# The first chunk's first two pairs of feed-forward products, issued among attention's last groups

## The chip, the cores and the metric

One core of a Trainium2 chip runs the whole program in one launch. The metric is the device time in microseconds, from the first to the last instruction of the core, and less is better. TensorE (PE) does the matrix products, with a queue of its own for loading weights (PEld); VectorE (DVE), ScalarE (ACT) and GpSimd (POOL) do the rest; SyncE (SP) issues most of the DMAs. Each engine is given its own list of instructions, and the lists meet only at semaphores.

## The reference

One transformer layer on x of 4096 tokens by 256 channels, all in float32:

```python
q, k, v = split_heads(x @ Wq.T + bq), ...      # 16 heads of 16
q, k = rope(q), rope(k)
att = softmax(where(tril, q @ k.T / 4, -inf))
x1 = layernorm(x + (att @ v) @ Wo.T + bo)
h = silu((x1 @ w1.T) * s1) * ((x1 @ w2.T) * s2)   # 256 -> 1024
h = gelu((h @ h1.T) * hs1)                        # 1024 -> 1024
h = gelu((h @ h2.T) * hs2)                        # 1024 -> 1024
out = layernorm(x1 + (h @ w3.T) * s3)             # 1024 -> 256
```

## The kernel before

The program has four stages, one behind the other on every engine: `project` (q, k, v), `attend` (attention), `widen` (the feed-forward layers w1/w2 and h1) and `narrow` (h2, w3 and the last norm).

**Attention.** The work is cut into 32 blocks (4 quads of heads, 8 chunks of 512 queries) and 576 groups of 128 keys; the last quad goes through its chunks from the longest to the shortest, so that its last blocks have 12, 8 and 4 groups. In a group PE computes four key units (`key_unit`, lines 513 and 516, three banks `at_key`), ACT turns each into probabilities with Exp (line 648), and PE multiplies the probabilities of the group before by the values (`values`, line 532, bank `at_o`). Beside this PE computes row units (line 499, four banks `at_row`), whose maxima DVE takes. The row units run ahead of the keys: they end with group `rows_done` = 555, and from group 556 on the four row banks are free. When a block is complete, ACT copies `at_o` out (`take_out`, line 639) between two groups' probabilities, and SP stores it.

**The preparation of the first chunk** (class `Prepare`, for chunk 0, whose attention is complete early) is written into attention's last groups. DVE multiplies the attention's output by the inverse denominators (`scale`, L843, `fr_o`). PE multiplies by Wo in four pieces (`project`, L820), one behind each of groups 559 to 562, into row banks 0 and 1. DVE adds, normalises and writes x1 (`norm`, L859 to L876, with one step on POOL). PE transposes x1 behind group 571 (`turn`, L829), again into row banks 0 and 1. DVE splits the transposed x1 into a high and a low part (`split_x1t`, L884 and L886, tile `fr_x1t`) and splits w1 and w2 in the same manner (`split_weight`, L732 and L734).

**The feed-forward stage** (`widen`) goes through eight chunks. In a chunk there are eight pairs k of products: product w1 and product w2 for 128 hidden channels each, six matrix instructions of 512 columns apiece (L970), into banks 2(k mod 2) and 2(k mod 2)+1 of four. ACT applies Silu to the first bank of a pair (L1011), DVE multiplies it with the second (L1032, here called the gate) and splits the product in two more passes (L1036, L1038). From k = 2 on a pair's banks have to be free again:

```python
if k >= 2:
    pe.wait_ge(pair_taken, n * FK + k - 1)
```

Then come the eight products of the h1 layer (L970 too, but from `wi_h_h`), whose results ACT takes with Gelu (L1017). The h1 weights are loaded by SP in eight pieces after the last block's output has been stored, and DVE splits them: in the first chunk one piece behind the gate of k = 3, one behind that of k = 5, the rest behind k = 7. Silu, Gelu and Exp need different tables in ACT, and an ACT_TABLE_LOAD stands ahead of the first use of each.

Banks of PSUM: `project`, `attend` and `widen` each open their own tensors, on the same eight banks of the chip.

Of the kernel before, what the change touches and what calls it, by code (L numbers as in the profile page):

```python
# [57 lines left out]
def project(nc, block, keep, io, qp_d, kp_d, v_d, front):  # L58
# [6 lines left out]
    with ExitStack() as ctx:  # L65
# [20 lines left out]
        main_ps = [ctx.enter_context(nc.psum_tensor(f"pr_main{i}", [P, CH], F32)) for i in range(3)]  # L86
        rot_ps = [ctx.enter_context(nc.psum_tensor(f"pr_rot{i}", [P, CH], F32)) for i in range(2)]
# [263 lines left out]
def attend(nc, block, keep, io, qp_d, kp_d, v_d, max_d, o_d, front, prep, projected):  # L351
# [16 lines left out]
    with ExitStack() as ctx:  # L368
# [20 lines left out]
        row_ps = [ctx.enter_context(nc.psum_tensor(f"at_row{i}", [P, CH], F32)) for i in range(RING_R)]  # L389
# [94 lines left out]
        def _(pe):  # L484
# [57 lines left out]
            for g, (n, j) in enumerate(groups):  # L542
# [349 lines left out]
def widen(nc, block, keep, io, h2_d, front, prep, attended):  # L892

    with ExitStack() as ctx:
# [14 lines left out]
        fb = [ctx.enter_context(nc.psum_tensor(f"wi_f{i}", [P, CH], F32)) for i in range(4)]  # L909
# [4 lines left out]
        pair_ready = sem("pair_ready")  # L914
# [47 lines left out]
        def _(pe):  # L962
            def product(bank, w, moving, count, cols, made=None, before=0):

                m = 0
                for c in range(count):
                    if made is not None:
                        pe.wait_ge(made, before + c + 1)
                    for a, b in ((0, 0), (0, 1), (1, 0)):
                        last = nc.tensor.matmul(bank[:, :], w[a][:, c, cols], moving(b, c),  # L970
                                                start=(m == 0), stop=(m == 3 * count - 1))
                        m += 1
# [373 lines left out]
```

## Time and profile before

| | |
|---|---|
| three runs | 2834.88, 2837.89, 2838.22 us; median 2837.89 |
| profiled execution | 2839.76 us; its span 2837.9 us |
| PE busy | 2739.1 us, 97% of the span |
| DVE, ACT, POOL busy | 67%, 48%, 4% |
| mean granted TensorE clock | 0.982 |
| attention ends, feed-forward begins on PE | 1806.3 and 1807.2 us from the span's start |

The profile lists, for every instruction, when it started, how long it took, how long its engine had been idle and what ended that idle time. Times below are counted from the span's start. A busy PE is counted with modelled ends, so that where products stand close behind one another only their starts say what one costs.

### The profile page before, as it was taken

The numbers are of one execution on the slowest core, as the hardware profiler recorded it, in microseconds if no ns is written. First come the engines' busy times: TensorE is split into PE (matmuls) and PEld (weight loads), VectorE is DVE, ScalarE is ACT, GpSimd is POOL, SyncE is SP. The second block draws the span as 40 slices with busy tenths as digits, with TensorE's granted clock in tenths as the row PEclk, the third lists the DMA queues.
The fourth block names the chain that finished last, engine by engine and source line by source line (L and its number), as shares of the span: only waits on it lengthen the run. The fifth ranks groups of instructions, "written<-read, shape, count | busy, mean of one in ns | idle before, by whom it ended". The sixth has DMA issues, their size and how long they took to land.

```text
span 2837.9 us, 39313 instructions
## 1 busy us (share of the span) xinstructions
PE 2739.1 (97%) x14880; PEld 1429.8 (50%) x14880; DVE 1902.2 (67%) x4001; ACT 1350.5 (48%) x2641; POOL 112.4 (4%) x151
## 2 busy tenths in 40 slices
PE   8889899999999999999999999999999998999998
PEld 4423233333333333333333332588888887888886
DVE  7889799888888887888887775633333352443343
ACT  3426566777776776777777776411211111001100
POOL 3302000010000020000000000000000000000000
PEclk9979899999999999999999999999999999999999
DMA  7734400017000053000001000311111132111100
GB/s 207 192 79 61 63 3 3 3 23 86 3 4 5 6 63 56 5 3 3 1 3 39 19 3 10 105 67 57 57 60 58 42 126 102 45 63 70 44 15 23
DMA packets 94732, 133.46 MB, mean 47 GB/s; under 512 B 30582, under 2 KB 68214, under 8 KB 90838
## 3 DMA queue, kind: packets, MB, share of 16 engines
q1 hardware_dynamic: 81436, 96.25, 10.6%
q0 software_dynamic: 5472, 23.34, 6.7%
q10 hardware_dynamic: 7648, 11.54, 1.4%
q8 instruction: 108, 1.77, 0.3%
q14 instruction: 68, 0.56, 0.1%
HBM read 83.77 MB, written 47.32 MB: 46 GB/s over the span
## 4 chain that ended last, share of the span: by engine, by line
PE 68%; issue 21%; DVE 6%; DMA 2%; ACT 1%; ACTq 1%; SPq 0%; POOL 0%; another core or an unknown queue 0%; POOLq 0%; DVEq 0%
PE at_o L532 18%; PE at_row L499 16%; PE at_key L513 15%; PE wi_f L970 15%; DVE at_segmax L584 3%; DVE fr_masked L580 1%; ACT at_probs L648 1%; DMA maxima<-at_maxrows 1%; PE at_key L516 1%; PE wi_p L820 1%; PE pr_main L130 1%; DVE pr_parts L251 1%; PE pr_rot L141 1%; PE pr_v L151 0%; DVE pr_full L247 0%
## 5 line engine op out<-in xcount | busy, mean ns | idle before, releaser
L648 ACT ACTIVATE at_probs<-at_key 128x512 f32<-128x512 f32 (+3 forms) x2304 | 1128.0, 567 | 523.6 <-PE at_key L513 367.9
L584 DVE TENSOR_REDUCE at_segmax<-at_row 128x1 f32<-128x512 f32 x1792 | 1143.1, 684 | 183.4 <-PE at_row L499 179.3
L513 PE MATMUL at_key<-fr_q_stack,fr_k_stack 99*128 99x512 bf16 (+3 forms) x1152 | 416.3, 366 | 14.9 <-DMA fr_q_stack<-maxima 10.6
L499 PE MATMUL at_row<-fr_k_stack,fr_q_stack 96*128 96x512 bf16 (+3 forms) x1152 | 406.0, 377 | 19.1 <-POOL at_values L429 13.3
L513 PE MATMUL at_key<-at_q_stack,at_k_stack 99*128 99x512 bf16 (+3 forms) x1152 | 403.9, 366 | 6.9 <-ACT at_probs L648 6.3
L499 PE MATMUL at_row<-at_k_stack,at_q_stack 96*128 96x512 bf16 (+3 forms) x1152 | 408.7, 365 | 1.7 <-DVE at_segmax L584 1.1
L532 PE MATMUL at_o<-at_probs,at_values 128*32 128x512 f32 (+3 forms) x2304 | 288.7, 574 | 0.0
L532 PE MATMUL at_o<-at_probs,fr_values 128*32 128x512 f32 (+3 forms) x2304 | 287.9, 572 | 0.0
L580 DVE CUSTOM_DVE_ANT_0 fr_masked<-at_row,fr_causal 128x384 f32<-128x384 f32 (+3 forms) x512 | 243.7, 483 | 54.7 <-PE at_row L499 54.3
L499 PEld LDWEIGHTS at_row<-fr_k_stack,fr_q_stack 96*128 96x128 bf16 x1152 | 110.6, 99 | 316.9 <-DVE at_segmax L584 159.7
L499 PEld LDWEIGHTS at_row<-at_k_stack,at_q_stack 96*128 96x128 bf16 x1152 | 110.8, 98 | 307.7 <-DVE at_segmax L584 163.5
L1205 ACT ACTIVATE na_h3f<-na_h,na_hs 128x512 f32<-128x512 f32 x64 | 44.1, 690 | 405.8 <-PE na_h L1175 405.8
L1175 PE MATMUL na_h<-na_h_h,fr_h2w_h 128*128 128x512 f32 x512 | 203.8, 398 | 9.0 <-DVE na_h_l L1220 9.0
L1175 PE MATMUL na_h<-na_h_l,fr_h2w_h 128*128 128x512 f32 x512 | 203.6, 398 | 0.0
L1175 PE MATMUL na_h<-na_h_h,fr_h2w_l 128*128 128x512 f32 x512 | 203.4, 397 | 0.0
L970 PE MATMUL wi_f<-wi_h_h,wi_h1w_h 128*128 128x512 f32 x512 | 201.4, 393 | 0.0
L970 PE MATMUL wi_f<-wi_h_l,wi_h1w_h 128*128 128x512 f32 x512 | 199.3, 389 | 0.0
L970 PE MATMUL wi_f<-wi_h_h,wi_h1w_l 128*128 128x512 f32 x512 | 199.3, 389 | 0.0
L1017 ACT ACTIVATE wi_h<-wi_f,fr_hs 128x512 f32<-128x512 f32 x64 | 44.1, 689 | 324.6 <-PE wi_f L970 324.6
L1227 DVE CAST na_h_h<-na_h3f 128x512 fp32r<-128x512 f32 x64 | 27.3, 426 | 246.1 <-ACT na_h3f L1205 246.1
L513 PEld LDWEIGHTS at_key<-at_q_stack,at_k_stack 99*128 99x128 bf16 x1152 | 111.8, 98 | 158.0 <-ACT at_probs L648 95.1
L513 PEld LDWEIGHTS at_key<-fr_q_stack,fr_k_stack 99*128 99x128 bf16 x1152 | 113.0, 98 | 112.6 <-ACT at_probs L648 37.2
(116 smaller groups left out, 2733.5 us busy)
## 6 DMA issues: line engine op xcount, KB each, us to landing
hidden<-wi_h SPq DMA_DIRECT2D x64, 256.0 KB, 2.0
na_h2f<-hidden SPq DMA_DIRECT2D x8, 1024.0 KB, 7.7
q_parts<-pr_parts SPq DMA_DIRECT2D x48, 128.0 KB, 2.4
k_parts<-pr_parts SPq DMA_DIRECT2D x48, 128.0 KB, 3.3
at_q_stack<-q_parts POOLq DMA_DIRECT2D x48, 128.0 KB, 23.7
at_k_stack<-k_parts POOLq DMA_DIRECT2D x12, 512.0 KB, 28.1
values<-pr_vals SPq DMA_DIRECT2D x32, 136.0 KB, 4.1
outputs<-at_outs SPq DMA_DIRECT2D x128, 34.0 KB
```

The costliest lines, as they stand in the source:

```text
L130: last = nc.tensor.matmul(main_ps[g % 3][:, :], w[m // DH][:, c, cols], xt[:, n % BUFS, c, :], start=(c == 0), stop=(c == DH - 1))
L141: nc.tensor.matmul(rot_ps[g % 2][:, :], turn[:, :], lin[:, g % 3, :], start=True, stop=True).then_inc(rot_ready, 1)
L499: last = nc.tensor.matmul(bank[:, 0:w], qst[u][0:SROWS, c, h, i * P:(i + 1) * P], kst[u][0:SROWS, h, s * CH:s * CH + w], start=True, stop= ...
L513: last = nc.tensor.matmul(bank[:, q0:CH], kst[u][0:SROWS + PARTS, h, j * P:(j + 1) * P], qst[u][0:SROWS + PARTS, c, h, q0:CH], start=True, ...
L532: last = nc.tensor.matmul(o_ps[32 * h:32 * h + 32, q0:CH], vq[u][:, at:at + 32], probs[:, g % RING_P, h, q0:CH], start=(j == 0), stop=(g = ...
L580: nc.vector.tensor_tensor_reduce(out=masked[:, diagonal[r] % 2, 0:w], in0=row_ps[r % RING_R][:, 0:w], in1=causal[:, CH - w:CH], scale=1.0, ...
L584: nc.vector.tensor_reduce(segmax[:, n % 2, h * TPC + i, s:s + 1], row_ps[r % RING_R][:, 0:w], op=ALU.max, axis=AX.X).then_inc(rows_taken, 1)
L648: nc.scalar.activation(probs[:, g % RING_P, h, q0:CH], key_ps[m % RING_K][:, q0:CH], ACT.Exp).then_inc(probs_ready, 1)
L970: last = nc.tensor.matmul(bank[:, :], w[a][:, c, cols], moving(b, c), start=(m == 0), stop=(m == 3 * count - 1))
L1017: nc.scalar.activation(h2[:, k % 2, :], fb[k % 4][:, :], ACT.Gelu, scale=front.hs[:, k:k + 1]).then_inc(hid_taken, 1)
L1175: last = nc.tensor.matmul(hb[k % 4][:, :], h2w[a][:, c, cols], h2[b][:, c, :], start=(m == 0), stop=(m == 3 * FK - 1))
L1205: nc.scalar.activation(h3f[:, k % 2, :], hb[k % 4][:, :], ACT.Gelu, scale=hs[:, k:k + 1]).then_inc(hid_taken, 1)
```

## The change

PE now issues the pairs k = 0 and k = 1 of chunk 0 behind attention's groups 569 and 572, and `widen` starts chunk 0 with k = 2. The four banks that were `at_row`, `wi_f` and so on in the separate stages are one set, `front.banks`, for the whole program, and the chip's banks stay the same as before. The preparation uses only banks 2 and 3, with Wo's products behind groups 557 to 560 and the transposes behind group 566, since pair 0 writes banks 0 and 1, and pair 1 banks 2 and 3. On DVE the split of w1 stands ahead of the norm, and that of w2 ahead of `split_x1t`. The number of instructions stays as it was. ACT's and DVE's code for Silu and gate doesn't move: it still stands behind their part of attention.

```diff
+EARLY_PAIRS = 2
...
-        row_ps = [ctx.enter_context(nc.psum_tensor(f"at_row{i}", [P, CH], F32)) for i in range(RING_R)]
+        row_ps = front.banks
...
-                i = g - rows_done - 4
-                if i == 0:
+                after = g - rows_done
+                if after == 2:
                     pe.wait_ge(rows_taken, len(rows))
-                if 0 <= i < TPC:
-                    prep.project(pe, 0, i, row_ps[i // 2])
-                if i == 12:
-                    prep.turn(pe, 0, row_ps)
+                if 2 <= after < 2 + TPC:
+                    prep.project(pe, 0, after - 2, row_ps[2 + (after - 2) // 2])
+                if after == 11:
+                    prep.turn(pe, 0, row_ps[2:4])
+                if after in (14, 17):
+                    pe.wait_ge(prep.x1t_ready, DH)
+                    pe.wait_ge(prep.w_split, 4)
+                    first_layer(nc, pe, front, 0, (after - 14) // 3)
             values(NG - 1)
...
-            prep.norm(dve, 0, row_ps)
-            for i, (high, low) in enumerate((front.w1, front.w2)):
-                dve.wait_ge(prep.w_loaded[i], 16)
-                split_weight(dve, high[:, :, :], low[:, :, :], front.w_raw[i][:, :, :], prep.w_split, 2 * i)
-                if i == 0:
-                    prep.split_x1t(dve, 0, row_ps)
+            dve.wait_ge(prep.w_loaded[0], 16)
+            split_weight(dve, front.w1[0][:, :, :], front.w1[1][:, :, :], front.w_raw[0][:, :, :], prep.w_split, 0)
+            prep.norm(dve, 0, row_ps[2:4])
+            dve.wait_ge(prep.w_loaded[1], 16)
+            split_weight(dve, front.w2[0][:, :, :], front.w2[1][:, :, :], front.w_raw[1][:, :, :], prep.w_split, 2)
+            prep.split_x1t(dve, 0, row_ps[2:4])
...
+def first_layer(nc, pe, front, n, k):
+
+    cols = slice(k * P, (k + 1) * P)
+    x1t = front.x1t[n % 2]
+    product(nc, pe, front.banks[2 * (k % 2)], front.w1, lambda b, c: x1t[:, b, c, :], DH, cols)
+    product(nc, pe, front.banks[2 * (k % 2) + 1], front.w2, lambda b, c: x1t[:, b, c, :], DH, cols).then_inc(front.pair_ready, 1)
...
-                for k in range(FK):
-                    cols = slice(k * P, (k + 1) * P)
+                for k in range(EARLY_PAIRS if n == 0 else 0, FK):
                     if k >= 2:
                         pe.wait_ge(pair_taken, n * FK + k - 1)
                     elif n > 0:
                         pe.wait_ge(hid_taken, (n - 1) * FK + 6 + 2 * k)
-                    product(fb[2 * (k % 2)], front.w1, lambda b, c: x1t[:, b, c, :], DH, cols)
-                    product(fb[2 * (k % 2) + 1], front.w2, lambda b, c: x1t[:, b, c, :], DH, cols).then_inc(pair_ready, 1)
+                    first_layer(nc, pe, front, n, k)
```

How this stands in the engines' queues. On PE, before, values of group 568 are followed straight by the keys of group 570 (`at_o` is the values' bank, 32x512 x4 the four heads):

```order
L513 MATMUL at_key<-at_q_stack,at_k_stack 128x384
L516 MATMUL at_key<-at_mask,at_ident 128x128
L532 MATMUL at_o<-at_probs,at_values 32x512 x4
L513 MATMUL at_key<-at_q_stack,at_k_stack 128x256
L516 MATMUL at_key<-at_mask,at_ident 128x128
L513 MATMUL at_key<-at_q_stack,at_k_stack 128x256
```

In the change the same place, behind group 569, holds the twelve instructions of pair 0 (L744 is `product`, 4 rows of 3; `fr_bank` is the common name of the four banks):

```order
L533 MATMUL at_o<-at_probs,at_values 32x512 x4
L744 MATMUL fr_bank<-fr_x1t_66,fr_w_h 128x512 x2
L744 MATMUL fr_bank<-fr_x1t_66,fr_w_l 128x512
L744 MATMUL fr_bank<-fr_x1t_66,fr_w_h 128x512 x2
L744 MATMUL fr_bank<-fr_x1t_66,fr_w_l 128x512
L744 MATMUL fr_bank<-fr_x1t_66,fr_w_h 128x512 x2
L744 MATMUL fr_bank<-fr_x1t_66,fr_w_l 128x512
L744 MATMUL fr_bank<-fr_x1t_66,fr_w_h 128x512 x2
L744 MATMUL fr_bank<-fr_x1t_66,fr_w_l 128x512
L514 MATMUL at_key<-at_q_stack,at_k_stack 128x256
L517 MATMUL at_key<-at_mask,at_ident 128x128
L514 MATMUL at_key<-at_q_stack,at_k_stack 128x256
```

Pair 1 stands in the same way behind group 572. What moved is the order alone: both pairs come from the stage's boundary, which on PE looked as follows before (values of groups 574 and 575, the branch into `widen`, pair 0):

```order
L513 MATMUL at_key<-at_q_stack,at_k_stack 128x128
L516 MATMUL at_key<-at_mask,at_ident 128x128
L532 MATMUL at_o<-at_probs,at_values 32x256 x4
L532 MATMUL at_o<-at_probs,at_values 32x128 x4
L961 UNCONDITIONAL_BRANCH
L970 MATMUL wi_f<-fr_x1t_66,fr_w_h 128x512 x2
L970 MATMUL wi_f<-fr_x1t_66,fr_w_l 128x512
L970 MATMUL wi_f<-fr_x1t_66,fr_w_h 128x512 x2
```

In the change the row behind the branch is the first of pair k = 2, which waits for `pair_taken`:

```order
L514 MATMUL at_key<-at_q_stack,at_k_stack 128x128
L517 MATMUL at_key<-at_mask,at_ident 128x128
L533 MATMUL at_o<-at_probs,at_values 32x256 x4
L533 MATMUL at_o<-at_probs,at_values 32x128 x4
L988 UNCONDITIONAL_BRANCH
L744 MATMUL fr_bank<-fr_x1t_66,fr_w_h 128x512 x2
L744 MATMUL fr_bank<-fr_x1t_66,fr_w_l 128x512
```

The names are the same as before, but this pair stands behind no other product of the stage. On DVE, before, the preparation of chunk 0 stood in this order (L859 to L876 are the norm, L732 and L734 a weight's split, L884 and L886 the split of x1):

```order
L843 TENSOR_TENSOR fr_o<-fr_o,fr_recip 128x512 x2
L859 TENSOR_TENSOR fr_x_61<-at_row,fr_bo 128x256 x4
L862 TENSOR_TENSOR fr_x_61<-fr_x_61,fr_x 128x1024
L865 BN_STATS fr_stats<-fr_x_61 128x6 x4
L870 BN_AGGR fr_mv<-fr_stats 128x2 x4
L873 TENSOR_SCALAR fr_var<-fr_mv 128x4
L876 TENSOR_SCALAR fr_x_61<-fr_x_61,fr_mv,fr_rstd 128x256 x4
L732 CAST fr_w_h<-fr_w_raw 128x2048
L734 TENSOR_TENSOR fr_w_l<-fr_w_raw,fr_w_h 128x2048
L884 CAST fr_x1t_66<-at_row 128x512
```

In the change the first weight's split comes ahead of the norm, and the second weight's ahead of x1's:

```order
L870 TENSOR_TENSOR fr_o<-fr_o,fr_recip 128x512 x2
L759 CAST fr_w_h<-fr_w_raw 128x2048
L761 TENSOR_TENSOR fr_w_l<-fr_w_raw,fr_w_h 128x2048
L886 TENSOR_TENSOR fr_x_61<-fr_bank,fr_bo 128x256 x4
L889 TENSOR_TENSOR fr_x_61<-fr_x_61,fr_x 128x1024
L892 BN_STATS fr_stats<-fr_x_61 128x6 x4
L897 BN_AGGR fr_mv<-fr_stats 128x2 x4
L900 TENSOR_SCALAR fr_var<-fr_mv 128x4
L903 TENSOR_SCALAR fr_x_61<-fr_x_61,fr_mv,fr_rstd 128x256 x4
L759 CAST fr_w_h<-fr_w_raw 128x2048
L761 TENSOR_TENSOR fr_w_l<-fr_w_raw,fr_w_h 128x2048
L911 CAST fr_x1t_66<-fr_bank 128x512
```

So all that the two early pairs read is ready once the last of these rows and the two or three behind it are done; the rows of `widen` that follow on DVE are unchanged.

## Rows read from the trace of the kernel before

**Rows 1.** Busy time, share of the span, instructions, from the page

```profile
PE 2739.1 (97%) x14880; PEld 1429.8 (50%) x14880; DVE 1902.2 (67%) x4001; ACT 1350.5 (48%) x2641; POOL 112.4 (4%) x151
```

**Rows 2.** Timeline of PE: start, us, engine, line, operands [idle before <-what ended it]

```profile
1805.40 0.86 PE L532 MATMUL at_o<-at_probs,at_values 128*32 128x256 f32 x16
1807.19 0.71 PE L970 MATMUL wi_f<-fr_x1t,fr_w_h 128*128 128x512 f32 x2 [0.92 <-ACT at_outs L639]
...
1813.09 0.72 PE L970 MATMUL wi_f<-fr_x1t,fr_w_h 128*128 128x512 f32 x2 [0.15 <-DVE wi_gated L1032]
...
1824.51 0.74 PE L970 MATMUL wi_f<-fr_x1t,fr_w_h 128*128 128x512 f32 x2 [0.15 <-DVE wi_gated L1032]
...
1830.13 0.47 PE L970 MATMUL wi_f<-wi_h_h,wi_h1w_h 128*128 128x512 f32 x1
```

**Rows 3.** Timeline of ACT around the boundary of the stages

```profile
1806.33 0.60 ACT L639 ACTIVATE at_outs<-at_o 128x512 f32<-128x512 f32 x1 [0.54 <-PE at_o L532]
1810.27 1.28 ACT L1011 ACT_TABLE_LOAD   x1 [3.33 <-PE wi_f L970]
1811.56 0.69 ACT L1011 ACTIVATE wi_silu<-wi_f,fr_s 128x512 f32<-128x512 f32 x1
...
1830.33 0.69 ACT L1011 ACTIVATE wi_silu<-wi_f,fr_s 128x512 f32<-128x512 f32 x1 [2.06 <-PE wi_f L970]
1831.04 1.28 ACT L1017 ACT_TABLE_LOAD   x1
```

**Rows 4.** Timeline of DVE in chunk 0 of the feed-forward stage

```profile
1812.29 0.75 DVE L1032 SCALAR_TENSOR_TENSOR wi_gated<-wi_f,fr_s,wi_silu 128x512 f32<-128x512 f32 x1 [8.64 <-ACT wi_silu L1011]
...
1814.14 0.75 DVE L1032 SCALAR_TENSOR_TENSOR wi_gated<-wi_f,fr_s,wi_silu 128x512 f32<-128x512 f32 x1
...
1821.48 0.69 DVE L732 CAST wi_h1w_h<-wi_h1w_raw 128x1024 fp32r<-128x1024 f32 x1
...
1823.81 0.65 DVE L1032 SCALAR_TENSOR_TENSOR wi_gated<-wi_f,fr_s,wi_silu 128x512 f32<-128x512 f32 x1
```

**Rows 5.** The h1 weights' tile, first piece: issue and landing (ns min/median/max, then us)

```profile
L934 SPq DMA_DIRECT2D wi_h1w_raw<-in_h1T x1: 400/400/400, 1814.8 to 1814.8; - x1
...
DMA to landing us min/median/max: 4.3/4.3/4.3
```

**Rows 6.** Timeline of PE at the starts of groups 558, 567, 569, 570, 573, 574

```profile
1760.25 0.82 PE L513 MATMUL at_key<-at_q_stack,at_k_stack 99*128 99x512 bf16 x3
...
1785.93 0.82 PE L513 MATMUL at_key<-at_q_stack,at_k_stack 99*128 99x512 bf16 x3
...
1790.96 0.34 PE L513 MATMUL at_key<-at_q_stack,at_k_stack 99*128 99x384 bf16 x1
...
1793.32 0.28 PE L513 MATMUL at_key<-at_q_stack,at_k_stack 99*128 99x256 bf16 x1
...
1799.61 0.34 PE L513 MATMUL at_key<-at_q_stack,at_k_stack 99*128 99x384 bf16 x1
...
1802.54 0.28 PE L513 MATMUL at_key<-at_q_stack,at_k_stack 99*128 99x256 bf16 x1
```

**Rows 7.** Timeline of DVE in the preparation of chunk 0

```profile
1759.44 1.29 DVE L843 TENSOR_TENSOR fr_o<-fr_o,fr_recip 128x512 f32<-128x512 f32 x2 [8.25 <-DMA fr_recip<-denominators]
...
1776.07 0.76 DVE L859 TENSOR_TENSOR fr_x<-at_row,fr_bo 128x256 f32<-128x256 f32 x2 [5.35 <-PE at_row L820]
...
1784.02 2.29 DVE L734 TENSOR_TENSOR fr_w_l<-fr_w_raw,fr_w_h 128x2048 fp32r<-128x2048 f32 x1
1797.45 0.69 DVE L884 CAST fr_x1t<-at_row 128x512 fp32r<-128x512 f32 x1 [11.14 <-PE at_row L829]
```

**Rows 8.** Stretches: length, busy of PE, PEld, DVE, ACT, POOL, granted clock, DMA

```profile
1748.00:1751.00 3.00, 1.07 (x7) 0.34 (x4) 1.67 (x8) 0.37 (x1) 0.00 (x0) 0.90 0.06 22
1751.00:1758.00 7.00, 7.00 (x25) 1.17 (x24) 0.18 (x1) 4.13 (x8) 0.00 (x0) 0.56 0.16 38
1781.00:1785.00 4.00, 4.00 (x17) 0.69 (x21) 3.50 (x6) 2.41 (x6) 0.43 (x1) 0.57 0.06 16
```

More of the change, by code:

```diff
@@ L85, in project @@
         vals = sb("vals", [P, 2, 2, HEADS, VW])
-        main_ps = [ctx.enter_context(nc.psum_tensor(f"pr_main{i}", [P, CH], F32)) for i in range(3)]
-        rot_ps = [ctx.enter_context(nc.psum_tensor(f"pr_rot{i}", [P, CH], F32)) for i in range(2)]
+        main_ps = front.banks[0:3]
+        rot_ps = [front.banks[3], ctx.enter_context(nc.psum_tensor("pr_rot1", [P, CH], F32))]
         v_ps = [ctx.enter_context(nc.psum_tensor(f"pr_v{i}", [P, 2, D], F32)) for i in range(2)]
@@ L709, in __init__ @@
         self.rstd = place("rstd", at + 48, [P, TPC])
+        self.banks = [ctx.enter_context(nc.psum_tensor(f"fr_bank{i}", [P, CH], F32)) for i in range(RING_R)]
+        self.pair_ready = sem("pair_ready")
         self.consts_loaded = sem("consts_loaded")
@@ L727, in load_first, with product @@
             queue.dma_start(self.kst[part, :, c * CH:(c + 1) * CH], k_v[ka, 0, :, c]).then_inc(self.first_loaded[c], 16)
+def product(nc, pe, bank, w, moving, count, cols, made=None, before=0):
+    m = 0
+    for c in range(count):
+        if made is not None:
+            pe.wait_ge(made, before + c + 1)
+        for a, b in ((0, 0), (0, 1), (1, 0)):
+            last = nc.tensor.matmul(bank[:, :], w[a][:, c, cols], moving(b, c), start=(m == 0), stop=(m == 3 * count - 1))
+            m += 1
+    return last
+def first_layer(nc, pe, front, n, k):
[3 more added lines that the diff above has]
+    product(nc, pe, front.banks[2 * (k % 2) + 1], front.w2, lambda b, c: x1t[:, b, c, :], DH, cols).then_inc(front.pair_ready, 1)
 def split_weight(dve, high, low, raw, split, done):
@@ L908, in widen @@
         h2 = sb("h2", [P, 2, CH])
-        fb = [ctx.enter_context(nc.psum_tensor(f"wi_f{i}", [P, CH], F32)) for i in range(4)]
+        fb = front.banks
         pb = [ctx.enter_context(nc.psum_tensor(f"wi_p{i}", [P, CH], F32)) for i in range(2)]
@@ L913, in widen @@
         h1w_split = sem("h1w_split")
-        pair_ready = sem("pair_ready")
+        pair_ready = front.pair_ready
         silu_ready = sem("silu_ready")
@@ L962, in _ @@
         def _(pe):
[L963 to L972, printed above, removed]
-                return last
             pe.wait_ge(prep.w_split, 4)
@@ L1001, in _ @@
                         pe.wait_ge(hid_taken, n * FK + k - 3)
-                    product(fb[k % 4], h1w, lambda b, c: h1[b][:, c, :], FK, slice(k * P, (k + 1) * P),
+                    product(nc, pe, fb[k % 4], h1w, lambda b, c: h1[b][:, c, :], FK, slice(k * P, (k + 1) * P),
                             h1_ready if k == 0 else None, FK * n).then_inc(hid_ready, 1)
@@ L1087, in narrow @@
         rstd = sb("rstd", [P, TPC])
-        hb = [ctx.enter_context(nc.psum_tensor(f"na_h{i}", [P, CH], F32)) for i in range(4)]
+        hb = front.banks
         yb = [ctx.enter_context(nc.psum_tensor(f"na_y{i}", [P, CH], F32)) for i in range(2)]
```

1 line of the change is left out of this document (removed).

## The prediction

> **What bounds the kernel now.** I begin with the page's busy time: PE works 97% of the span [rows 1], so the question is where PE's remaining idle time lies and whether the change removes or adds some. Then comes PE's timeline at the boundary of the two stages [rows 2]. The last value product begins at 1805.40 and ends 0.86 us later, at 1806.26; I call this point E and count from it. Pair 0 begins at E+0.93, after 0.92 us idle that ended with ACT's copy of the last block. From there to the first h1 product at 1830.13 (E+23.87) PE stops twice more for DVE's gate, 0.15 us by the row each time, before k = 2 and k = 6. That is all the idle time that there is to win at this place, about 1.2 us.
>
> A pair costs PE 2.8 us: from 1813.09 to 1824.51 are four pairs, 11.42 less one stop of 0.15, over four = 2.82 [rows 2].
>
> The third view is ACT's timeline [rows 3]. ACT ends the copy at 1806.93 (E+0.67), then sits idle for 3.33 us until pair 0 is complete, then loads the Silu table (1.28 us), then applies Silu. So today the two pairs are PE's cover for a serial chain: last copy, table, Silu, gate. The fourth view is DVE's timeline [rows 4]: the first gate ends at 1812.29 + 0.75 = 1813.04 and PE starts k = 2 at 1813.09.
>
> **The change: the moved products.** 24 matrix instructions go from behind E to ahead of it. Does attention hide them? In this part PE is the engine that others wait for: ACT's probabilities start when a key unit is done, and PE adds the pair between two groups, with no key of the next group issued meanwhile. The group after it still has to wait for its own first probability. So I count 2 x 2.8 = 5.6 us in full there, and the same 5.6 us leaves `widen`: zero. One exception: group 573 takes 1802.54 - 1799.61 = 2.93 us since ACT inserts a block's copy, where group 569 with the same widths takes 1793.32 - 1790.96 = 2.36 [rows 6]. Pair 1 stands right ahead of group 573, and ACT copies meanwhile: -0.57.
>
> **The change: the preparation.** Wo's first product moves from behind group 559 to behind group 557, which ends at 1760.25 [rows 6]. DVE's scaling, which it needs, ends at 1759.44 + 1.29 = 1760.73 [rows 7]. PE, and with it attention, waits: +0.5. The other three pieces and the transposes only change places. Is x1 ready for the transposes? With groups of 2.5 us and 1.0 us per piece, piece 4 is done at 1772.2. Before, from the norm's second half to the end of one weight's split passed 1784.02 + 2.29 - 1776.07 = 10.2 us [rows 7]. Norm and second split are thus done by 1782.6; the transposes come at 1785.93 + 0.5 [rows 6, 7]. They take 1 us, and four passes of 0.69 us [rows 7] end by 1790.3. Pair 0 comes at 1793.32 + 0.5 + 1.0 = 1794.8. The margin is 4.5 us, so these waits cost nothing. The first split hides in the time in which DVE waits for Wo's products. New end of attention: E' = E + 5.6 + 0.5 - 0.6 = E + 5.5.
>
> **The change: what lies bare behind E'.** PE now meets k = 2 directly, and k = 2 waits for gate 0. Behind gate 0 stand, from E': copy done at +0.67; table load at once, as at 1831.04, which starts 0.02 us behind the Silu that ended at 1831.02, done +1.97; Silu 0.70, done +2.67; gate with its start +0.79, done +3.45; PE starts at +3.50 [rows 3, 4]. The idle time of 0.93 becomes 3.5 us. Queued behind this waiting instruction is everything of `widen`; nothing of attention's work is left to fill it.
>
> The next thing that is late is the h1 weights. Their first piece is issued at 1814.78 (E+8.52, once the last output is stored) and lands 4.3 us later [rows 5], at E+12.8. That time goes along with E'. DVE splits this piece behind gate 3 and ahead of gate 4. PE does k = 2 and 3 from E'+3.5 in 2.8 us each. Silu can begin 3.08 us after a pair's start (1810.27 - 1807.19) [rows 2, 3]. Pair 3 starts at +6.3, gate 3 at +10.1, and its two splits end 1.85 later (the distance of two gates) [rows 4], at +12.0. DVE then waits for the piece until +12.85. From the start of the split to PE's restart passed 1824.51 - 1821.48 = 3.03 us [rows 2, 4]: k = 6 can't start before E'+15.9, where PE would be ready at 3.5 + 4 x 2.8 = 14.7. Two more pairs: h1 products begin at E'+21.5. Gate 6, which they need too, comes at the same moment, so I add nothing.
>
> **Sum.** E' + 21.5 - (E + 23.87) = 5.5 + 21.5 - 23.9 = +3.1 us. In the terms of the idle time: +2.6 at the boundary, +1.0 at k = 6 net of the old stops, +0.5 scaling, -0.6 copy, the rest rounding.
>
> **The clock.** No row shows a stop of 3.5 us here. The nearest one is the 1.9 us for which PE was not busy between 1748 and 1751 [rows 8]: in the 7 us behind it the mean granted clock was 0.56, so 2 x 0.44 x 7 = 6.2 us went by at the lower level (1.2 GHz, where 1.00 is 2.4 GHz). Between 1781 and 1785 there is a spell of 2 x 0.43 x 4 = 3.4 us. At half clock PE loses half of it: 1.7 to 3.1 us. But k = 6 waits anyway. DVE had 0.85 us to spare at the weights (12.85 against 12.0), and PE 1.2 us: a loss L behind the stop moves k = 6 by L - 0.85, so by 0.8 or 2.2 us. If the spell begins while PE still waits, less. I take 1.3, bounds 0 and 2.2.
> Expected: 3.1 + 1.3 = +4.4 us. On the profiled execution's own 2839.76 this is 2844.2. That execution stands 1.9 us above the median of the runs, so for the median 2837.89 + 4.4 = 2842.3.
>
> The Trainium skill ("TensorE: Matmul & The Clock Gate", section "Why this matters for your kernels") says that idle gaps between bursts of matmuls send PE back to half clock; by that rule the fall comes, and rows 8 agree in kind.
> The Trainium skill ("ScalarE: Activation LUTs", section "What ACT_TABLE_LOAD costs") adds a drain of about 1.38 us to each load of 1.283 us. By this rule gate 0, and with it k = 2, comes 1.38 us later; beside the clock's loss, which has used up the margin, that would make +5.8. The load at 1831.04 stands 0.02 us behind the Silu before it and the Silu at 1811.56 follows its load without a gap [rows 3], so the trace shows no such time on either side, and I leave it out.
>
> **Rivals.**
> 1. *Bare chain with a clock spell* (the forecast): +3.1 and 0.8 to 2.2. Chance 0.58, own range 2840 to 2844.5.
> 2. *Bare chain without the price at k = 6 and without a clock loss*: the last output is stored sooner and DVE finds the weights there. +3.1 - 1.0 to +3.1, say +2.5: 2840.4. For it: a landing of 4.3 us is one sample. Against it: DVE reaches the piece 0.85 us too early by my count. Chance 0.17.
> 3. *A longer chain*: something sits between copy and Silu that today's 3.33 us of idle time hide, like the code behind the branch, or a second spell of low clock. Each 1.4 us counts in full: +5.8 to +7.5, 2843.7 to 2845.4. Rows 3 show that the chain's parts follow one another within 0.04 us, but not this sequence. Chance 0.17.
> 4. *The other side*: attention's last groups hide the pairs. It needs PE's time in these groups to be slack, as it would be if ACT were the bound. The price is then -5.6 instead of 0: 3.1 - 5.6 = -2.5, 2835.4; it decides from 3.1 of the 5.6 us hidden (4.4 with the clock's loss). ACT does stand busy for most of such a group, which speaks for it. Against it: ACT was idle 0.54 us even ahead of its last copy, and PE and ACT wait for each other in turn within a group. Chance 0.05.
> 5. *The preparation is late* and PE stands inside attention ahead of pair 0. Past the margin of 4.5 us each us costs one; a norm 6.5 us late gives +6.4, 2844.3. Chance 0.03.
>
> **Numbers.** A difference within 0.2% (5.7 us) can't be told from no change. Most of 1 and 2 lies within it; a quarter of 1 with the runs' own scatter (2834.88 to 2838.22), most of 3 and half of 5 lie above: 0.3 slower, 0.66 same, 0.04 faster, from 4. The range 2839.0 to 2846.0 takes in 1 to 3 with that scatter.
>
> **What the profile after would show.** PE's first instruction of `widen` (k = 2) about 3.5 us behind the last value product, released by DVE's gate, with ACT's copy, table load and Silu in one unbroken row. PE idle 0.5 us ahead of Wo's first product. No idle time ahead of the early pairs. A DVE wait for the first h1 piece and a PE stop of about a microsecond, less under a low clock, at k = 6. Granted clock under 1 in the 7 us behind the boundary. Wrong would be: a group with a pair less than 2.8 us longer, or ACT's table loaded before the last copy, which would shorten the chain by 1.28 us.

## The result, and the profile after

| | median of ten runs | lowest to highest |
|---|---|---|
| before | 2837.55 us | 2830.64 to 2839.86 |
| the change | 2845.6 us | 2841.66 to 2846.85 |

The ratio is 1.0027, 95% interval 1.0018 to 1.0035: +7.7 us (5.1 to 9.9), slower. I had given a difference within 0.2% (5.7 us) the chance 0.66; the interval's lower end still lies inside it. The median lies inside the range, 3.3 us above my 2842.3. The number that I had forecast, +4.4, lies outside the interval. One later execution of the change took 4657.59 us at a mean clock of 0.654; it is in no comparison below. The profiled execution took 2841.66 us (span 2839.8), the lowest of its ten and only 1.9 us above the profiled execution before; so one pair of profiles shows less than the medians do, and the question behind the result is where the rest comes from.

The page of the change: busy time, share, instructions.

```profile
PE 2740.6 (97%) x14880; PEld 1432.6 (50%) x14880; DVE 1902.1 (67%) x4001; ACT 1349.8 (48%) x2641; POOL 112.0 (4%) x151
```

As many products as before [rows 1], and PE's busy time is up by 1.5 us: no work was added. The timeline of PE (start, us, operands, idle time and what ended it): the last block's transposed maxima, Wo's first product, the two early pairs, the last value products, k = 2, the first h1 product:

```profile
1749.90 0.27 PE L494 MATMUL fr_bank<-at_ident,at_maxparts 128*48 128x128 bf16 x1 [1.94 <-DVE at_maxparts L605]
...
1760.18 1.10 PE L847 MATMUL fr_bank<-fr_wo,fr_o 128*128 128x256 f32 x4 [0.55 <-DVE fr_o L870]
...
1792.94 0.72 PE L744 MATMUL fr_bank<-fr_x1t,fr_w_h 128*128 128x512 f32 x2
...
1801.17 0.74 PE L744 MATMUL fr_bank<-fr_x1t,fr_w_h 128*128 128x512 f32 x2
...
1809.28 0.86 PE L533 MATMUL at_o<-at_probs,at_values 128*32 128x256 f32 x16
1813.73 0.70 PE L744 MATMUL fr_bank<-fr_x1t,fr_w_h 128*128 128x512 f32 x2 [3.59 <-DVE wi_gated L1044]
...
1826.71 0.73 PE L744 MATMUL fr_bank<-fr_x1t,fr_w_h 128*128 128x512 f32 x2
...
1832.33 0.46 PE L744 MATMUL fr_bank<-wi_h_h,wi_h1w_h 128*128 128x512 f32 x1
```

It answers to [rows 2, 6]. Attention ends at E' = 1809.28 + 0.86 = 1810.14; k = 2 starts 3.59 us later, and DVE's gate released it. The first h1 product stands at E' + 22.19 (before: E + 23.87). The two pairs stand without any idle time in front, and the keys behind them come 2.86 and 2.88 us after a pair's start. ACT and DVE behind the boundary, which answer to [rows 3, 4]:

```profile
1810.21 0.60 ACT L644 ACTIVATE at_outs<-at_o 128x512 f32<-128x512 f32 x1 [0.55 <-PE at_o L533]
1810.82 1.28 ACT L1023 ACT_TABLE_LOAD   x1
1812.12 1.26 ACT L1023 ACTIVATE wi_silu<-fr_bank,fr_s 128x512 f32<-128x512 f32 x2
```

```profile
1812.84 0.75 DVE L1044 SCALAR_TENSOR_TENSOR wi_gated<-fr_bank,fr_s,wi_silu 128x512 f32<-128x512 f32 x1 [24.77 <-ACT wi_silu L1023]
...
1821.83 0.75 DVE L1044 SCALAR_TENSOR_TENSOR wi_gated<-fr_bank,fr_s,wi_silu 128x512 f32<-128x512 f32 x1 [0.82 <-ACT wi_silu L1023]
...
1823.68 0.69 DVE L759 CAST wi_h1w_h<-wi_h1w_raw 128x1024 fp32r<-128x1024 f32 x1
...
1826.01 0.65 DVE L1044 SCALAR_TENSOR_TENSOR wi_gated<-fr_bank,fr_s,wi_silu 128x512 f32<-128x512 f32 x1
```

Copy, table and two Silus stand in one row, each start at most 0.04 us behind the end before it. DVE splits the first h1 piece at 1823.68, right behind the splits of gate 3 (1821.83 + 1.85): it didn't wait for the weights. The stretches of the clock, as in [rows 8] (the column behind POOL is the mean granted clock, 1.00 full and 0.50 half speed):

```profile
1750.00:1758.00 8.00, 7.93 (x28) 1.40 (x27) 0.28 (x1) 4.54 (x9) 0.00 (x0) 0.59 0.18 41
1814.00:1820.00 6.00, 6.00 (x21) 4.73 (x20) 3.42 (x7) 0.69 (x1) 0.00 (x0) 0.72 0.21 65
```

Behind the boundary 2 x 0.28 x 6 = 3.4 us went by at half clock. I call such a time a spell. The first stretch, ahead of Wo's products, holds a spell as in the profile before, and it proved to be the key to the rest.

### The profile page after: what moved, and what is told of

It is laid out like the page before. It is cut to its first block, busy times and chain, and to the rows that moved or that the text cites. A ratio compares the mean times of both kernels' runs of the same rounds, so it can differ in the third digit from the quotient of the medians.

```text
span 2839.8 us, 39315 instructions
## 1 busy us (share of the span) xinstructions
PE 2740.6 (97%) x14880; PEld 1432.6 (50%) x14880; DVE 1902.1 (67%) x4001; ACT 1349.8 (48%) x2641; POOL 112.0 (4%) x151
## 4 chain that ended last, share of the span: by engine, by line
PE 68%; issue 21%; DVE 6%; DMA 1%; ACT 1%; ACTq 1%; SPq 0%; POOL 0%; another core or an unknown queue 0%; POOLq 0%; DVEq 0%
PE at_o L533 17%; PE fr_bank L500 16%; PE fr_bank L744 15%; PE at_key L514 15%; DVE at_segmax L589 3%; DVE fr_masked L585 1%; ACT at_probs L653 1%; PE at_key L517 1%; DMA maxima<-at_maxrows 1%; PE wi_p L847 1%; PE fr_bank L131 1%; PE pr_v L152 1%; DVE pr_parts L252 0%; DVE pr_full L248 0%; PE pr_rot L142 0%
## 5 line engine op out<-in xcount | busy, mean ns | idle before, releaser
L589 DVE TENSOR_REDUCE at_segmax<-fr_bank 128x1 f32<-128x512 f32 x1792 | 1143.3, 684 | 180.5 <-PE fr_bank L500 176.2
L500 PE MATMUL fr_bank<-fr_k_stack,fr_q_stack 96*128 96x512 bf16 (+3 forms) x1152 | 406.6, 378 | 19.0 <-POOL at_values L430 13.3
L500 PE MATMUL fr_bank<-at_k_stack,at_q_stack 96*128 96x512 bf16 (+3 forms) x1152 | 408.8, 365 | 1.8 <-DVE at_segmax L589 1.1
L585 DVE CUSTOM_DVE_ANT_0 fr_masked<-fr_bank,fr_causal 128x384 f32<-128x384 f32 (+3 forms) x512 | 243.8, 483 | 55.1 <-PE fr_bank L500 54.7
L1187 PE MATMUL fr_bank<-na_h_h,fr_h2w_h 128*128 128x512 f32 x512 | 203.9, 398 | 9.2 <-DVE na_h_l L1232 9.0
L1187 PE MATMUL fr_bank<-na_h_l,fr_h2w_h 128*128 128x512 f32 x512 | 203.3, 397 | 0.0
L1187 PE MATMUL fr_bank<-na_h_h,fr_h2w_l 128*128 128x512 f32 x512 | 203.2, 397 | 0.0
L744 PE MATMUL fr_bank<-wi_h_h,wi_h1w_h 128*128 128x512 f32 x512 | 201.6, 394 | 0.0
L744 PE MATMUL fr_bank<-wi_h_h,wi_h1w_l 128*128 128x512 f32 x512 | 199.6, 390 | 0.0
L744 PE MATMUL fr_bank<-wi_h_l,wi_h1w_h 128*128 128x512 f32 x512 | 199.6, 390 | 0.0
```

Source lines behind the costliest of these rows:

```text
L500: last = nc.tensor.matmul(bank[:, 0:w], qst[u][0:SROWS, c, h, i * P:(i + 1) * P], kst[u][0:SROWS, h, s * CH:s * CH + w], start=True, stop= ...
L585: nc.vector.tensor_tensor_reduce(out=masked[:, diagonal[r] % 2, 0:w], in0=row_ps[r % RING_R][:, 0:w], in1=causal[:, CH - w:CH], scale=1.0, ...
L589: nc.vector.tensor_reduce(segmax[:, n % 2, h * TPC + i, s:s + 1], row_ps[r % RING_R][:, 0:w], op=ALU.max, axis=AX.X).then_inc(rows_taken, 1)
L1187: last = nc.tensor.matmul(hb[k % 4][:, :], h2w[a][:, c, cols], h2[b][:, c, :], start=(m == 0), stop=(m == 3 * FK - 1))
```

## Experiments

Every experiment was compared with the kernel before on the same chip, and rows 1 to 4, 5 to 8 and 9 to 11 of the table have the runs of before in common. Microseconds are the ratio minus one, times the median of before there (2838.3 to 2838.8). The intervals are 2 to 3 us wide to either side, so differences between two rows of less than that are read from the profiles.

| kernel | ratio (95%) | us |
|---|---|---|
| the kernel before once more | 0.9997 (0.9987 to 1.0007) | -0.9 |
| the change once more | 1.003 (1.002 to 1.0041) | +8.5 |
| preparation only, no early pair | 1.0011 (1.0002 to 1.0019) | +3.1 |
| one early pair | 1.002 (1.0011 to 1.0028) | +5.7 |
| the preparation's places back, no early pair | 0.9999 (0.999 to 1.0008) | -0.3 |
| both pairs one group later, Wo's products two | 1.0016 (1.0007 to 1.0025) | +4.5 |
| the change, PE kept busy in the stop | 1.0024 (1.0014 to 1.0034) | +6.8 |
| the change, Silu's table loaded ahead of the copy | 1.0029 (1.0018 to 1.004) | +8.2 |
| before, pair 0 doesn't wait for the copy | 0.9994 (0.9985 to 1.0003) | -1.7 |
| the same, last maxima one group later | 0.9984 (0.9975 to 0.9993) | -4.5 |
| the change, last maxima one group later | 1.0028 (1.0017 to 1.0038) | +7.9 |

### Is the difference real?

Two kernels without an edit: the one before, and the change.

> The kernel before, run as if it were a change, to see how far two sets of runs of one kernel lie apart. Expected: within 2 us of the kernel before, and an interval that holds 1. If it lies 3 us or more away, part of the +8.0 us between the two medians is scatter.

> The changed kernel again. The first comparison gave medians 8.0 us apart, while the profiled executions stood only 1.9 us apart. Theory A (a bare chain of 3.5 us and a clock spell behind it, +4.4 by my sum): +3 to +6 us. Theory B (something beside the boundary of the stages adds 3 us or more, which my sum lacks): +7 to +9 us again. The profile is to show the stop of about 3.5 us in any case.

The kernel before lies within 1 us of itself. The change is at +8.5 us (5.7 to 11.6) again. So +4.4 missed something: 4 us by this run, 1.3 us by the lower end of its interval. Theory A alone was too small. The profile of the kernel before once more shows the reason, though I understood it only beside the next one. The last maxima on PE, and a stretch of seven microseconds that begins a microsecond later:

```profile
1754.95 0.22 PE L493 MATMUL at_row<-at_ident,at_maxparts 128*48 128x128 bf16 x1 [1.93 <-DVE at_maxparts L600]
```

```profile
1756.00:1763.00 7.00, 6.13 (x36) 1.39 (x36) 0.00 (x0) 5.83 (x13) 0.00 (x0) 1.00 0.20 44
```

The same stop of 1.9 us as in the execution that I had predicted from, but no spell at half clock behind it (1.00 against 0.56 in [rows 8]). From the maxima's product to the end of attention this execution needs 52.3 us. The execution that I had predicted from needs 55.7: its maxima's product stands at 1750.59, and it had two spells on the way, both in [rows 8].

### Preparation alone, one pair alone

The first kernel has the edit below; the second has 1 in place of 0.

```diff
-EARLY_PAIRS = 2
+EARLY_PAIRS = 0
...
-                if after in (14, 17):
+                if after in (14, 17)[:EARLY_PAIRS]:
```

> The changed kernel with both pairs back in the feed-forward stage; shared banks, the preparation on banks 2 and 3, its earlier places and the new order on VectorE stay. Theory A: only the wait ahead of Wo's first product is left, +0.5 us, and the stop at the boundary is 0.9 us as before. Theory B (the shared banks or the preparation cost the time): +3 us or more.

> The changed kernel with only pair 0 issued early (behind group 569); pair 1 comes first in the feed-forward stage. Theory A: TensorE has pair 1 (2.8 us) as cover for the chain of copy, table load, Silu and gate, whose end at 3.5 us meets TensorE's end of pair 1 at 0.9 + 2.8 = 3.7 us; no stop of 3.5 us, no spell at half clock from it; +0.5 us for the scaling and up to +1.0 at k = 6 for the h1 weights: +0.5 to +1.5 us. Theory B: as much slower as with both pairs, +4 us or more.

The preparation alone costs 3.1 us (0.6 to 5.4), not 0.5: theory A failed at this step. One pair costs 5.7 us (3.1 to 7.9), outside theory A's +0.5 to +1.5 as well. The timeline of PE with the preparation alone, and its stretches:

```profile
1750.89 0.22 PE L494 MATMUL fr_bank<-at_ident,at_maxparts 128*48 128x128 bf16 x1 [1.93 <-DVE at_maxparts L605]
...
1761.12 2.05 PE L847 MATMUL fr_bank<-fr_wo,fr_o 128*128 128x256 f32 x4 [2.65 <-DVE fr_o L870]
```

```profile
1752.00:1759.00 7.00, 5.66 (x33) 1.18 (x33) 0.00 (x0) 5.72 (x12) 0.00 (x0) 1.00 0.21 45
1761.00:1768.00 7.00, 6.88 (x21) 2.96 (x22) 3.40 (x2) 2.06 (x4) 0.00 (x0) 0.55 0.00 0
```

PE stands 2.65 us ahead of Wo's first product, and waits for DVE's scaling. Here too no spell followed the stop at the maxima (clock 1.00), so PE came to Wo's product two microseconds earlier than in my profile, while the scaled output came no earlier. Then, behind the new stop, PE ran at a mean clock of 0.55 for 7 us. With one pair the same stop is 2.63 us long:

```profile
1765.56 2.05 PE L847 MATMUL fr_bank<-fr_wo,fr_o 128*128 128x256 f32 x4 [2.63 <-DVE fr_o L870]
```

From the end of attention to the first h1 product pass 21.50 us, against 23.86 with no early pair, and the stop at the boundary is 0.92 us, as before. So a single pair leaves no stop of 3.5 us there. In attention the pair takes 2.88 us, so in the profile it costs 2.88 - 2.36 = +0.5 us, within what theory A allows it. That theory missed the time, and theory B's "+4 us or more" met it, since both kernels have the stop ahead of Wo's product. The medians' difference of 2.6 us between the two kernels is larger than 0.5, but their intervals overlap.

Why doesn't the scaled output come earlier, when PE does? SP's timeline in the kernel before, and the step of DVE that makes the inverse denominators ready:

```profile
1751.21 0.31 SPq L446 DMA_DIRECT2D maxima<-at_maxrows  x1
1752.57 0.23 SPq L450 DMA_DIRECT2D at_q_stack<-maxima  x1
1752.85 0.35 SPq L798 DMA_DIRECT2D denominators<-pp_den  x1
1754.43 3.54 SPq L804 DMA_DIRECT2D fr_recip<-denominators  x8
```

```profile
1737.32 0.55 DVE L835 RECIPROCAL pp_den<-pp_den 128x64 f32<-128x64 f32 x1
```

The denominators are ready at 1737.87, but in SP's list their store stands behind the last maxima's store and reload, and so behind the maxima's product on PE. The end of the scaling follows that product by 10.0 to 10.3 us in all thirteen profiles. PE at full clock needs only 7.6 us to Wo's place behind group 557 (1761.12 - 2.65 - 1750.89). With a spell of 6.8 us it needed 9.7 (1760.18 - 0.55 - 1749.90 = 9.73), and 0.5 us of the wait was left. Whether an earlier place of that store in SP's list would take the wait away was not tried.

### Back to the old places

The first kernel has no early pair, and Wo's products and the transposes where they were before (the diff, against the change). The second moves both pairs along instead: the transposes behind group 12 and the pairs behind groups 15 and 18, in the count of the loop.

```diff
-EARLY_PAIRS = 2
+EARLY_PAIRS = 0
...
-                if 2 <= after < 2 + TPC:
-                    prep.project(pe, 0, after - 2, row_ps[2 + (after - 2) // 2])
-                if after == 11:
+                if 4 <= after < 4 + TPC:
+                    prep.project(pe, 0, after - 4, row_ps[2 + (after - 4) // 2])
+                if after == 16:
...
-                if after in (14, 17):
-                    pe.wait_ge(prep.x1t_ready, DH)
-                    pe.wait_ge(prep.w_split, 4)
-                    first_layer(nc, pe, front, 0, (after - 14) // 3)
```

> Shared banks, the preparation on banks 2 and 3 and the new order on VectorE, but no early pair, Wo's products back behind groups 559 to 562 and the transposes back behind group 571. Theory C (formed from the last runs): in the kernel with the preparation alone TensorE stood 2.65 us ahead of Wo's first product and then ran 6.8 us at half clock, because Wo's products come two groups (about 5 us) too early for the denominators that come back from memory; the profile that I predicted from had a clock spell just before, which hid all but 0.5 us of it. By C this kernel has no such wait and lies within 1 us of the kernel before. Rival D (shared banks or the order on VectorE cost the time): +3 us as with the preparation alone.

> Both pairs early, but Wo's products behind groups 559 to 562, the transposes behind 567 and the pairs behind 570 and 573. Theory C: no wait ahead of Wo's first product, so the change's +8.5 loses the 3.1 us of the preparation: +5 to +6 us, and what is left is the bare chain at the boundary (stop of 3.6 us instead of 0.9) with its clock spell. Rival D: +8 us again.

Without pairs and with the old places nothing is left of the loss (-0.3 us, -2.8 to 2.3), and the profile shows no wait ahead of Wo's product:

```profile
1751.85 0.22 PE L494 MATMUL fr_bank<-at_ident,at_maxparts 128*48 128x128 bf16 x1 [1.94 <-DVE at_maxparts L601]
...
1764.28 0.92 PE L843 MATMUL fr_bank<-fr_wo,fr_o 128*128 128x256 f32 x3
...
1803.32 0.86 PE L533 MATMUL at_o<-at_probs,at_values 128*32 128x256 f32 x16
```

Its first h1 product follows the maxima's product by 76.19 us, as in the kernel before once more (1831.14 - 1754.95 = 76.19; neither had a spell). So shared banks and DVE's order cost nothing that these profiles show, and D's +3 us is out. With both pairs and the later places the loss is 4.5 us (2.0 to 7.1), which is what theory A had said for the whole change, and a little under the 5 to 6 expected here. Its maxima's product and its boundary:

```profile
1752.83 0.22 PE L494 MATMUL fr_bank<-at_ident,at_maxparts 128*48 128x128 bf16 x1 [1.93 <-DVE at_maxparts L605]
...
1810.04 0.86 PE L533 MATMUL at_o<-at_probs,at_values 128*32 128x256 f32 x16
1814.49 1.19 PE L744 MATMUL fr_bank<-fr_x1t,fr_w_h 128*128 128x512 f32 x2 [3.60 <-DVE wi_gated L1044]
...
1832.82 0.46 PE L744 MATMUL fr_bank<-wi_h_h,wi_h1w_h 128*128 128x512 f32 x1
```

Maxima to end of attention is 58.1 us here and 52.3 in the kernel without pairs, neither with a spell in this stretch: two pairs cost attention 5.7 us in full, 2.87 each. That rules out the rival by which attention hides them. The end of attention to the first h1 product is 21.9 against 23.9 us. 5.7 - 1.9 = +3.8 us.

### The clock behind the stop, and the chain

```diff
-            for name in ("probs_ready", "out_taken"):
-                pe.wait_ge(*attended[name])
+            pe.wait_ge(*attended["probs_ready"])
+            for _ in range(14):
+                nc.tensor.matmul(pb[0][:, :], front.w1[0][:, 0, 0:P], front.x1t[0][:, 0, 0, :], start=True, stop=True)
+            pe.wait_ge(*attended["out_taken"])
```

> The changed kernel with 14 additional products of 512 columns between the last value product and pair 2, into a bank that nobody reads there; they fill the stop of 3.6 us with 3.2 us of work and change nothing that is computed. They make nothing arrive earlier. Theory A2 (the clock spell behind the stop costs 0.8 us): no spell at half clock behind the boundary, and from the end of attention to the first h1 product 21.5 us instead of 22.2. Rival (the spell is fully hidden by the wait for h1 weights and gates): 22.2 us as before. Time: +7 to +8.5 us.

The timeline of PE and the stretch of 12 us from the end of attention on:

```profile
1812.33 0.86 PE L533 MATMUL at_o<-at_probs,at_values 128*32 128x256 f32 x16
1813.13 3.49 PE L993 MATMUL wi_p<-fr_x1t,fr_w_h 128*128 128x512 f32 x14
1816.80 0.71 PE L744 MATMUL fr_bank<-fr_x1t,fr_w_h 128*128 128x512 f32 x2 [0.18 <-DVE wi_gated L1046]
...
1835.00 0.47 PE L744 MATMUL fr_bank<-wi_h_h,wi_h1w_h 128*128 128x512 f32 x1
```

```profile
1812.00:1824.00 12.00, 11.70 (x64) 8.93 (x65) 6.22 (x10) 5.21 (x10) 0.00 (x0) 1.00 0.25 78
```

The stop is filled, the clock stays at 1.00, and the first h1 product comes 21.81 us after the end of attention instead of 22.19 (in the two profiles of the change 22.19 and 22.25), midway between the two values expected. So the spell at this place costs 0.4 us of the time up to that product. Where the rest of it goes can be read at k = 6. DVE's split of the first h1 piece, and PE's start of k = 6:

```profile
1826.08 0.69 DVE L759 CAST wi_h1w_h<-wi_h1w_raw 128x1024 fp32r<-128x1024 f32 x1 [0.84 <-DMA wi_h1w_raw<-in_h1T]
```

```profile
1829.39 0.73 PE L744 MATMUL fr_bank<-fr_x1t,fr_w_h 128*128 128x512 f32 x2 [1.36 <-DVE wi_gated L1046]
```

Without the spell DVE comes to the piece 0.84 us too early and PE stands for 1.36 us ahead of k = 6; with it both waits are gone. The kernel with one early pair, also without a spell there, shows the same two waits (0.60 and 0.97 us). The overall +6.8 can't be told from +8.5.

```diff
+        warm = sb("warm", [P, 1])
...
+                if g == NG - 1:
+                    act.wait_ge(prep.consts_loaded, prep.CONSTS)
+                    nc.scalar.activation(warm[:, :], front.s1[:, 0:1], ACT.Silu)
                 if g in out_after:
                     take_out(out_after[g])
```

> The changed kernel with a Silu of one column in ScalarE's list between the last Exp and the last copy, so that the table load stands ahead of the copy. The chain behind the last value product gets shorter: by the durations of the rows, the table is loaded at +0.8, the copy ends at +1.65, gate 0 at +3.1, and the stop is 3.15 instead of 3.6 us. But the last output is stored about 1.0 us later, and the h1 weights with it. If the chain alone counts: first h1 product 0.45 us sooner after the end of attention (21.8). If the weights bind at k = 6: not sooner, 22.2 to 22.6 us. Time: +8 to +9 us.

```profile
1814.13 0.86 PE L534 MATMUL at_o<-at_probs,at_values 128*32 128x256 f32 x16
1818.02 1.19 PE L748 MATMUL fr_bank<-fr_x1t,fr_w_h 128*128 128x512 f32 x2 [3.03 <-DVE wi_gated L1048]
...
1837.43 0.47 PE L748 MATMUL fr_bank<-wi_h_h,wi_h1w_h 128*128 128x512 f32 x1
```

The stop shrinks to 3.03 us, as the chain says, but the first h1 product comes at 1837.43, 22.44 us after the end of attention at 1814.99: not sooner. This execution had 6.8 us at half clock there (mean 0.57 over the 8 us from 1816), twice the 3.4 us of the change. DVE had no wait for the h1 weights there: it splits the first piece at 1828.79, right behind gate 3's own splits. So what held the first h1 product back was not the weights; the longer spell is what else differed. That the chain copy, table, Silu, gate sets the start of k = 2 is shown; that a shorter chain brings nothing is shown for this execution only.

### What else the boundary and the stop allow

```diff
-            for name in ("probs_ready", "out_taken"):
-                pe.wait_ge(*attended[name])
+            pe.wait_ge(*attended["probs_ready"])
...
+                    if n == 0 and k == 0:
+                        pe.wait_ge(*attended["out_taken"])
```

> The kernel before, only that pair 0 of the feed-forward stage no longer waits for ScalarE's last copy (its banks aren't the copied one); the wait stands ahead of the first h1 product. This takes what the change was after at the boundary, without moving a product. By the rows of before, the stop of 0.92 us goes and the first h1 product comes 22.9 instead of 23.9 us after the end of attention. Time: 0 to -1.5 us, which the comparison can't tell from nothing. Rival (the chain copy, table, Silu, gate bounds k = 2 anyway): 23.9 us as before, the stop moved to k = 2.

```diff
     assert r == len(rows)
+    done = before.index(len(rows))
+    for m in range(done, done + QUAD):
+        before[m] = len(rows) - 1
     return before
...
-                i = g - rows_done - 4
+                i = g - rows_done - 3
```

> The kernel of the last expectation, and the last block's transposed maxima (TensorE's wait of 1.93 us for VectorE) one group later, so that VectorE is done when TensorE arrives; Wo's products keep their groups. Theory C says that stops of 2 us at this place cost their own length and bring on spells at half clock in some executions: -2 to -5 us against the kernel before, no stop over 0.5 us there and no spell behind it. Rival (the spells come whatever TensorE does): -1.9 us at most.

> The changed kernel with the last block's maxima one group later. Theory C: TensorE reaches Wo's first product about 2 us sooner, but the scaled attention output comes no sooner, since it waits for the denominators from memory (and they are asked for one group later): the wait there grows to 4 us or more, and nothing is won, +7 to +10 us against the kernel before. Rival (the wait ahead of Wo is only a consequence of the clock): the stop disappears and the time falls by 2 to 5 us against the changed kernel.

The third kernel has the lines in `before` of the second on top of the change, and `after = g - rows_done + 1`, so that Wo's products stay in their groups.

The first kernel: pair 0 follows the last value product directly, and the first h1 product stands 23.06 us after the end of attention (23.87 before). The gain of 0.8 us is in the profile and lost in the scatter of the runs. The second kernel has the first one's edit too. Its maxima, Wo's first product and a stretch of 8 us:

```profile
1750.63 0.24 PE L496 MATMUL at_row<-at_ident,at_maxparts 128*48 128x128 bf16 x1
...
1761.06 1.10 PE L823 MATMUL at_row<-fr_wo,fr_o 128*128 128x256 f32 x4 [0.36 <-DVE fr_o L846]
```

```profile
1748.00:1756.00 8.00, 7.05 (x44) 1.72 (x41) 1.86 (x8) 6.25 (x13) 0.00 (x0) 1.00 0.09 25
```

No stop ahead of the maxima, clock 1.00, and -4.5 us (-7.1 to -2.0): this version beats both kernels, with 2.8 us of it from the maxima's place and 1.7 from the first edit, if the two rows of the table are taken at their middle values. The third kernel has the same repair on top of the change:

```profile
1749.75 0.24 PE L497 MATMUL fr_bank<-at_ident,at_maxparts 128*48 128x128 bf16 x1
...
1760.03 2.04 PE L850 MATMUL fr_bank<-fr_wo,fr_o 128*128 128x256 f32 x4 [5.13 <-DVE fr_o L873]
```

Here the 1.9 us that were won are handed straight back. PE stands 5.13 us ahead of Wo's product, and in its profile the mean clock over the 7 us from 1759 is 0.52. The kernel is as slow as the change (+7.9, 4.8 to 10.8). The stop is a wait for DVE's scaling. The scaling ends 10.1 us behind the maxima's product here too, and one group of 2.45 us less lies between that product and Wo's: 2.7 + 2.45 = 5.1 us of wait.

## Why the prediction was right, and where it fell short

**Direction and mechanism at the boundary** held. The pairs are no gain, since attention doesn't hide them and at the boundary they were the cover of a serial chain. The size did not hold: +4.4 against +7.7 (5.1 to 9.9) and +8.5 (5.7 to 11.6). That the median 2845.6 still fell into a range ending at 2846.0 is in part luck; the change's later runs have the median 2847.73, beside 2838.66 for the kernel before. The likeliest outcome, a difference within 0.2%, is missed by the median (0.27%), though the interval begins at 0.18%.

**The moved products**, counted at 5.6 us in full, measured 5.7 (maxima to the end of attention, both pairs against none). The 0.57 us that I took off for ACT's copy are in the profile of the change: the group behind pair 1 takes 2.36 us (its keys start at 1804.05 and those of the next group at 1806.41) where [rows 6] had 2.93. In the kernel with the later places pair 1 stands elsewhere, and the credit is gone. The terms named under the prediction's sum come to 3.5 us, not 3.1. More than half of the 0.4 that it calls rounding stems from 2.8 us for a pair: eight of them and the stops are 0.2 us short of the 23.87 of [rows 2].

**The chain**: 3.5 us predicted, 3.59 measured, with parts that follow one another as worked out. ACT's load shows no drain on either side, so the 1.38 us of the Trainium skill ("ScalarE: Activation LUTs", section "What ACT_TABLE_LOAD costs") are not in this chain: 1810.82 + 1.28 = 1812.10, and the Silu starts at 1812.12. Rival 3 falls for this reason. The Trainium skill puts such a drain beside every switch of tables; the measurement decides.

**k = 6**: predicted at E' + 15.9 without and 16.7 with a spell of 3.4 us; measured 1826.71 - 1810.14 = 16.57, with the spell and without a wait for the weights, since the spell had delayed gate 3 by more than the margin. Where the spell was kept away, k = 6 came at 1829.39 - 1813.19 = 16.20, and DVE waited 0.84 us for the weights where I had worked out 0.85. From E' to the first h1 product I had 21.5 and, with the spell, 22.3; measured 21.81 and 22.19.

**The clock behind the boundary**: I took 1.3 us. Filling the stop was worth 0.4. A spell of 3.4 us came in each of the four profiles that had the stop of 3.6 us unfilled.

**The preparation is the term that was mis-sized.** I wrote that PE "and with it attention, waits: +0.5". In the profile of the change it is 0.55, just as worked out, because that execution had the spell at half clock ahead of Wo's product again, and so had the second profile of the change (0.27). In three other profiles with Wo's product behind group 557 no spell preceded it, and the stop was 2.63 to 2.72 us, with 6.8 us at half clock behind it; in a fourth, with a spell of 3.4 us ahead, it was 1.59. Over many executions the preparation alone cost 3.1 us. I had read a cover from one execution and didn't say what it costs if that cover is gone. PE came to that place 2.1 us late in the execution that I had read (9.7 us behind the maxima's product instead of 7.6), while the end of the scaling is tied to the maxima's product. Without that delay the wait is 2.1 us longer, and a spell of its own follows.

What a spell costs can be read too, and it is less than the half that I had counted. From the maxima's product to the end of attention the kernel in which pair 0 doesn't wait for the copy needs 53.5 us with one spell of 3.4 us, and two kernels without any need 52.3: 1.2 us. With one early pair the same way takes 60.2 us; less 52.3, 2.9 for the pair and 2.6 for the stop, 2.4 us are left for 6.8 us at half clock. A part of the loss is made up where PE otherwise pauses for ACT. Two groups of the change, the first in the spell, the second behind it:

```profile
1753.87 1.97 PE L514 MATMUL at_key<-at_q_stack,at_k_stack 99*128 99x512 bf16 x4
...
1758.24 0.39 PE L514 MATMUL at_key<-at_q_stack,at_k_stack 99*128 99x512 bf16 x1 [0.32 <-ACT at_probs L653]
```

Eleven profiles have the stop of 1.9 us at the maxima: behind it 6.8 us at half clock in three, 3.4 us in two, nothing in six. The preparation costs 0.4 us in the first case (0.55 and 0.27), 1.6 + 1.2 = 2.8 in the second, 2.65 + 2.4 = 5.0 in the third. By this count, an estimate from few profiles, it costs 3.3 us in the mean, against 3.1 measured. The other terms, as measured, are 5.7 - 0.6 for the pairs and 22.2 - 23.9 = -1.7 up to the first h1 product. With 3.1 that makes +6.5, within both intervals; 4.5 for both pairs at the later places and 3.1 make +7.6.

The rival "a longer chain" (+5.8 to +7.5) came nearest in size but not in cause. The rival of a late preparation named the right stage and the wrong wait: I had checked the way from x1 to pair 0, which has time to spare in every profile with an early pair (no idle time ahead of it), and not the first wait of that way.

What stays open: why the stop of 1.9 us is followed by a spell in some executions and not in others, and how often over many.

## What to carry to other kernels

Work that is issued early on a serial engine is not hidden by that alone. Ask what it covered in its old place: here it was a chain copy, table load, activation, gate of 3.6 us. And before a wait is priced from a profile, look whether the waiting engine was late in that execution for a reason that isn't always there. A wait for data from memory that costs 0.5 us behind a spell at half clock cost 2.7 us and a spell of its own without it. It helps to count both sides of a wait from the event that releases them: here the data came 10.0 to 10.3 us behind one product on PE in every profile, and only PE's own way from there varied.

## What the runs showed of the hardware

Identical stops of TensorE, 1.93 us at the same product, were followed by 6.8 us, 3.4 us or nothing at half clock in different executions; the kernel before itself had 6.8 us in one profile and nothing in another. In this part of attention the price of such a stop was its length plus 2.2 to 2.4 us, 1.2 us or nothing. The kernel that removes this stop also has the narrower spread: 2831.27 to 2835.35 us over 11 runs, where the kernel with the stop and otherwise the same edit went from 2832.74 to 2841.39 over 11, and the kernel before beside them from 2832.46 to 2842.47 over 25. And products whose results nobody reads kept the clock at its upper level through a wait of 3.6 us, at no cost in time that the runs can tell (+6.8 us, 4.0 to 9.7, against +8.5).
